# Clearing the second block buffer of a recommendation tower with DMAs from DRAM in place of a ScalarE copy

## The chip, the core and the metric

The kernel runs on one core of a Trainium2 chip. Its engines are TensorE (PE in the profile; PEld is its weight load), VectorE (DVE), ScalarE (ACT), GpSimd (POOL) and SyncE (SP). Each works through its own list of instructions in order, and the lists wait for each other only through semaphores. SP issues the ordinary DMAs, POOL the indirect ones (gathers); both kinds run on the same 16 DMA engines, in queue q1 and queue q0 of the profile. The metric is device time in microseconds of one execution, the median of the runs.

## What is computed

For 512 samples: 50 embedding rows of 16 numbers are looked up, all pairwise inner products of the 50 rows are taken, and these 1225 numbers with 16 dense features go through a three-layer network.

```python
e = jnp.stack([tbl_0[ids[:, 0]], ..., tbl_49[ids[:, 49]]], axis=1)
gram = jnp.einsum('bid,bjd->bij', e, e)
z = gram[:, _I_IDX, _J_IDX]
h = jnp.concatenate([z, dense_ctx], axis=1)
h = jnp.maximum(h @ W_top1 + b_top1, 0.0)
h = jnp.maximum(h @ W_top2 + b_top2, 0.0)
y = h @ W_top3
```

## The kernel before

The samples are worked on in `TILES` = 4 tiles of 128, numbered t = 0 to 3. For each tile:

- **Small tables** (26 of them, and one larger) lie whole in SBUF. ACT makes one-hot rows (`onehots`), PE multiplies them with the tables (`select(t, u)`, `select_big(t)`), and DVE picks the wanted number out of each product (`pick`) and sums it up (`fold`).
- **Large tables** are read with one indirect DMA for each table and tile, issued by POOL: 11 "mid" and 12 "late" gathers for a tile, 92 in all, one after the other and without any wait but that for the ids. They write to `moving`; semaphores `mid_gathered[t]` and `late_gathered[t]` count them. The last six of tile 3 have a semaphore of their own.
- **Turning.** DVE transposes `moving` into `mcols` (`turn_mid(t)`, line 637, after the mid gathers; `turn_late(t)`, line 659, after the late ones) and the small tables' rows into `scols` (`turn_smalls(t)`).
- **Spreading.** The pairwise products of four groups of samples are done in one matmul against a block-diagonal operand, `blocks`, which has room for two tiles: `blocks[:, t % 2]`. Only the four diagonal blocks are ever written after the start (`diagonal`, line 222, called from `spread_mid` and `spread_late`, half by ACT and half by DVE). All the rest of it must be zero, so both halves of `blocks` are cleared once: the one for tiles 0 and 2 by DVE (line 530) and ACT (line 332) at the start, the one for tiles 1 and 3 by ACT alone, in the middle of tile 0's work.
- **Products.** PE multiplies: `product_y(t)` (line 860) after `spread_mid(t)`, `product_x(t)` (line 879) after `spread_late(t)` and ACT's `raise_late(t)` (line 420). ACT and DVE move the results to `z` (`unload_y`, `unload_x`, line 237), and PE runs the network: `first_layer` (line 886) and `second_layer`.

The orders on ACT, DVE and PE are written out by hand; the parts of the four tiles are interleaved. Around the change ACT's list reads

```python
            onehots(1, 1)
            place_lower(0)
            shift(0)
            clear(blocks[:, 1]).then_inc(zeroed[1], 1)
            raise_mid(0)
            spread_mid(0)
            onehots(1, 2)
            spread_late(0, 0, YS)
            raise_late(0, 0, YS)
```

SP's list issues all inputs of the first phase in one run: ids, small tables, the one-hot sources `wide`, `table_big`, 12 pieces of the first weight matrix, and the second layer's weights and biases. Then it waits until ACT is done with `onehots(1, 2)` before it issues the last `wide` load (`load_wide(3)`), for ACT's `onehots(3, 0)` in tile 1's work.

Of the kernel before, what the change touches and what calls it, by code (L numbers as in the profile page):

```python
# [8 lines left out]
P = 128  # L9
# [24 lines left out]
Q = 4  # L34
QP = P // Q
# [11 lines left out]
MS = YS + CH  # L47
# [13 lines left out]
WC = 9  # L61
NWC = -(-NS // WC)
NQ = NS + PARTS
NBC = -(-NQ // BC)
ROUND = 1.5 * 2 ** 23

# [13 lines left out]
def wide_groups(t):  # L80

    return [(NQ * u // NWC, NQ * (u + 1) // NWC) for u in range(NWC)]


def field_groups(size):

    return [(a, min(a + size, NQ)) for a in range(0, NQ, size)]

# [3 lines left out]
    return f if f < NS else W + f - NS  # L92


def build_tower(nc, quotients, ids, ids_t, extra, small, big, w1, w2, b2, w3, consts_in, ident_in, out, *tables):
    f32 = mybir.dt.float32
    bf16 = mybir.dt.bfloat16
    i32 = mybir.dt.int32
# [5 lines left out]
    with ctx:  # L104
        def sb(name, shape, dt=f32):
            return ctx.enter_context(nc.sbuf_tensor(name, shape, dt))
# [4 lines left out]
        def sem(name):  # L111
            return ctx.enter_context(nc.semaphore(name))
# [14 lines left out]
        quot_t = sb("quot_t", [P, B], bf16)  # L127
        wide = sb("wide", [P, 2, NQ * P], bf16)
        quot = sb("quot", [P, TILES, NS])
# [4 lines left out]
        mask_big = sb("mask_big", [P, TILES, BR])  # L134
        onehot = sb("onehot", [P, 2, NQ, P])
        square = sb("square", [P, BC * P])
# [5 lines left out]
        blocks = sb("blocks", [P, 2, QP, MS, Q])  # L142
# [44 lines left out]
        late_cols = sem("late_cols")  # L187
        mid_upper = sem("mid_upper")
        late_upper = sem("late_upper")
        zeroed = [sem(f"zeroed{n}") for n in range(2)]  # L190
        cleaned = sem("cleaned")
        mid_blocks = [sem(f"mid_blocks{n}") for n in range(2)]
        late_blocks = [sem(f"late_blocks{n}") for n in range(2)]
# [26 lines left out]
        def diagonal(copy, t, q, a, b):  # L220

            return copy(blocks[QP * q:QP * (q + 1), t % 2, :, a:b, q], mcols[QP * q:QP * (q + 1), t % 2, :, a:b])  # L222

        def share(t, side):

            n = Q // 2 if t < TILES - 1 else 1
            return range(n) if side == 0 else range(n, Q)
# [23 lines left out]
        @block.sync  # L251
        def _(sp):

            sp.dma_start(ids_sb[:, 0:NL], ids[:, 0:NL]).then_inc(first_loaded, 16)
            sp.dma_start(ids_t_sb[:], ids_t).then_inc(ids_t_loaded, 16)
            sp.dma_start(consts[:], consts_in).then_inc(consts_loaded, 16)
            sp.dma_start(ident[:], ident_in).then_inc(ident_loaded, 16)
            sp.dma_start(ids_sb[:, NL:], ids[:, NL:]).then_inc(ids_loaded, 16)

            def load_table(u):  # L260

                a, b = START[UNITS[u][0]], START[UNITS[u][1]]
                sp.dma_start(table[:, a:b], small[P * a:P * b, :].rearrange("(p c) o -> p (c o)", p=P)
                             ).then_inc(tables_loaded[u], 16)

            def load_wide(t):

                for a, b in wide_groups(t):
                    sp.dma_start(wide[:, t % 2, P * a:P * b], quotients[t:t + 1, P * a:P * b].to_broadcast([P, P * (b - a)])
                                 ).then_inc(wide_loaded[t], 16)  # L270

            for u in range(0, 3):
                load_table(u)
            sp.wait_ge(quot_ready, 1)
            by_field = quotients.rearrange("t (s b) -> s t b", s=NQ)
            sp.dma_start(by_field[0:NS], quot_t[0:NS, :].rearrange("s (t b) -> s t b", t=TILES)).then_inc(quot_stored, 16)
            sp.dma_start(by_field[NS:NQ], quot_t[W:W + PARTS, :].rearrange("s (t b) -> s t b", b=P)
                         ).then_inc(quot_stored, 16)
            for u in range(3, NSC):
                load_table(u)  # L280
            sp.wait_ge(quot_stored, 32)
            load_wide(1)
            for i in range(PARTS):
                sp.dma_start(table_big[:, i], big.rearrange("(i p r) d -> p i (r d)", i=PARTS, r=BR)[:, i]).then_inc(big_loaded, 16)
            load_wide(2)
            for c in range(CH):
                sp.dma_start(w1_sb[:, c], w1.rearrange("(c p) n -> p c n", p=P)[:, c]).then_inc(w1_loaded, 16)
            for side in range(2):
                sp.dma_start(z[SIDE * side + WIDE:SIDE * (side + 1)], extra[side:side + 1, 0:2]).then_inc(extra_loaded[0], 16)
            sp.dma_start(w2_sb[:], w2.rearrange("(k p) n -> p k n", p=P)).then_inc(w2_loaded, 16)  # L290
            sp.dma_start(b2_sb[:], b2.to_broadcast([3 * W, H2])).then_inc(w2_loaded, 16)
            sp.dma_start(w3_sb[:], w3.to_broadcast([P, H2])).then_inc(w2_loaded, 16)
            sp.wait_ge(onehot_ready, NBC + NWC)
            load_wide(3)
            for t in range(2, TILES):
                sp.wait_ge(sums_made, t - 1)
                for side in range(2):
                    sp.dma_start(z[SIDE * side + WIDE:SIDE * (side + 1), t % 2], extra[side:side + 1, t]
                                 ).then_inc(extra_loaded[t - 1], 16)
            sp.wait_ge(y_ready, TILES)  # L300
            sp.dma_start(out.rearrange("(p t) o -> p (t o)", t=TILES), y[:]).then_inc(stored, 16)
            sp.wait_ge(stored, 16)
# [20 lines left out]
        def _(act):  # L323
            def zeros(shape):

                n, m = shape
                return moving[:, 0, 0, 0:D].unsqueeze(1).unsqueeze(1).to_broadcast([P, n, m, D])

            def clear(part):

                to = part.rearrange("p j s q -> p (j s q)").rearrange("p (n m d) -> p n m d", m=2, d=D)
                return nc.scalar.copy(to, zeros((part.shape[1] * MS * Q // (2 * D), 2)))
# [1 line left out]
            act.wait_ge(padded, 1)  # L334
            nc.scalar.copy(fixed[:, :, UPPER:, D:], zeros((2, NS))).then_inc(cleaned, 1)
            nc.scalar.copy(fixed[:, :, 0:UPPER, 0:D], zeros((2, UPPER))).then_inc(cleaned, 1)
            clear(blocks[:, 0, QP // 2:]).then_inc(zeroed[0], 1)
            act.wait_ge(consts_loaded, 16)
            act.wait_ge(ident_loaded, 16)
            nc.scalar.copy(ident_bf[:], ident[:]).then_inc(selector_ready, 1)  # L340
# [44 lines left out]
            def spread_mid(t):  # L385

                act.wait_ge(mid_cols, t + 1)
                if t >= 2:
                    act.wait_ge(y_made, 2 * (t - 1))
                act.wait_ge(zeroed[t % 2], 2 - t % 2)  # L390
                for q in share(t, 0):
                    diagonal(nc.scalar.copy, t, q, YS, MS).then_inc(mid_blocks[0], 1)

# [9 lines left out]
            def spread_late(t, a, b):  # L403

                act.wait_ge(late_cols, t + (2 if a else 1))
                if t >= 2:
                    act.wait_ge(x_made, 2 * (t - 1))
                act.wait_ge(zeroed[t % 2], 2 - t % 2)
                for q in share(t, 0):
                    diagonal(nc.scalar.copy, t, q, a, b).then_inc(late_blocks[0], 1)  # L410

# [50 lines left out]
            onehots(1, 1)  # L462
            place_lower(0)
            shift(0)
            clear(blocks[:, 1]).then_inc(zeroed[1], 1)
            raise_mid(0)
            spread_mid(0)
            onehots(1, 2)
            spread_late(0, 0, YS)
# [46 lines left out]
        def _(dve):  # L516
# [10 lines left out]
            for n in range(3):  # L527
                nc.vector.memset(adder[W * n:W * n + 1], 1.0).then_inc(adder_ready, 1)
            step(nc.vector.memset(quot_t[:], 0.0))
            nc.vector.memset(blocks[:, 0, 0:QP // 2], 0.0).then_inc(zeroed[0], 1)  # L530
            dve.wait_ge(ids_t_loaded, 16)
            dve.wait_ge(consts_loaded, 16)
            step(nc.vector.tensor_scalar(quot_f[:], ids_t_sb[:], iota[0:W + PARTS, 3 + R + BR:4 + R + BR],
# [17 lines left out]
            for left, to, r in ((parts[0][1], masks[0], RS[0]), (parts[1][1], masks[1], RS[1])):  # L551
                n = to.shape[2]
# [86 lines left out]

            def spread_mid(t):  # L640

                dve.wait_ge(zeroed[t % 2], 2 - t % 2)
                dve.wait_ge(mid_cols, t + 1)
                if t >= 2:
                    dve.wait_ge(y_made, 2 * (t - 1))
                for q in share(t, 1):
                    diagonal(nc.vector.tensor_copy, t, q, YS, MS).then_inc(mid_blocks[1], 1)
# [13 lines left out]

            def spread_late(t, a, b):

                dve.wait_ge(zeroed[t % 2], 2 - t % 2)
                dve.wait_ge(late_cols, t + (2 if a else 1))
                if t >= 2:
                    dve.wait_ge(x_made, 2 * (t - 1))  # L667
                for q in share(t, 1):
                    diagonal(nc.vector.tensor_copy, t, q, a, b).then_inc(late_blocks[1], 1)
# [139 lines left out]
        def _(pe):  # L809
# [11 lines left out]
            def select(t, u):  # L821
# [7 lines left out]
                else:  # L829
                    pe.wait_ge(onehot_ready, NBC + NWC * (t - 1) + 1 + sum(end < b for _, end in wide_groups(t)))  # L830
                if t == 0:
# [6 lines left out]
            def select_big(t):  # L838

                m = first_unit(t) + NSC  # L840
                pe.wait_ge(rows_used, m - 1)
                pe.wait_ge(onehot_ready, NBC + NWC * t)
                pe.wait_ge(big_loaded, 16 * PARTS)
# [86 lines left out]
            def second_bias(t):  # L930

                if t == 0:
                    pe.wait_ge(w2_loaded, 48)
                    pe.wait_ge(bcast_used, NBC)
                    pe.wait_ge(bias_parts, 3)
# [172 lines left out]
```

## Time and profile before

| | us |
|---|---|
| median of 3 runs | 134.31 (133.75 to 134.5) |
| the profiled execution, own time | 134.14 |
| its span, first to last instruction | 132.3 |
| busy in the span: PE, PEld | 116.3, 105.6 |
| busy: DVE, POOL, ACT | 90.5, 87.8, 73.1 |

In the page's time line the span is cut into 40 slices of 3.3 us. Each digit is the busy share of a slice in tenths. The DMA row shows that the 16 DMA engines are full in slices 1 to 8 (to about 30 us), half full in slices 9 to 11, and almost empty after. PEclk is the clock that TensorE was granted; it lies lower in slices 8 to 10. A row of a timeline reads: start, duration, engine, line, operation, output<-input, shapes, and in brackets how long the engine had been idle and what released it.

### The profile page before, as it was taken

To read this page: it belongs to the slowest core of one execution; us is meant where nothing else is said; L and a number is where in the kernel's file an instruction comes from. 1 tells how busy PE (TensorE), PEld (TensorE's weight loads), DVE (VectorE), ACT (ScalarE), POOL (GpSimd) and SP (SyncE) were. 2 spreads that over 40 slices of the span, in tenths; PEclk is the share of its full clock that TensorE was granted. 3 is DMA by queue.
4 is the path that set the end of the run, shared out by engine and by line. 5 is a ranking of instruction groups with operands and counts; after the bars stand their busy time and mean duration, and the time that the engine had idled before them with its cause. 6 is when DMAs were issued, how large, how long until landed. Compare 5 with 4: busy or idle time off the path is not lost.

```text
span 132.3 us, 3154 instructions
## 1 busy us (share of the span) xinstructions
PE 116.3 (88%) x1266; PEld 105.6 (80%) x1266; DVE 90.5 (68%) x162; ACT 73.1 (55%) x106; POOL 87.8 (66%) x96
## 2 busy tenths in 40 slices
PE   0199699739999999999989999999989999998990
PEld 0189486529996999999976999997789999898980
DVE  5947857997977789984875599965959635424211
ACT  7765999999699659964521934012930142222210
POOL 2777877877877778777777787787787787750000
PEclk9999999975699999999999999999999999999999
DMA  2999999993530100001011000000010000010000
GB/s 40 260 265 294 380 380 368 373 338 75 185 130 10 10 10 7 5 7 16 5 7 12 5 7 7 10 11 6 9 12 5 7 12 5 7 12 0 5 0 1
DMA packets 9411, 10.92 MB, mean 83 GB/s; under 512 B 2667, under 2 KB 6411, under 8 KB 9395
## 3 DMA queue, kind: packets, MB, share of 16 engines
q1 hardware_dynamic: 6453, 9.96, 22.8%
q0 software_dynamic: 2944, 0.76, 5.7%
q8 instruction: 10, 0.16, 0.5%
q14 instruction: 4, 0.03, 0.1%
HBM read 10.68 MB, written 0.03 MB: 81 GB/s over the span
## 4 chain that ended last, share of the span: by engine, by line
POOL 65%; issue 21%; PE 6%; DMA 3%; DVE 2%; POOLq 1%; DVEq 0%
POOL moving L317 33%; POOL moving L312 32%; DMA moving<-tbl,ids_sb 2%; PE psm L886 2%; PE gram L879 2%; DMA ids_sb<-in_ids 1%; PE pt L949 1%; POOLq L104 1%; DVE blocks L222 1%; PE p L886 1%; PE gram L886 1%; DVE mcols L659 0%; DVE h2w L704 0%; DVEq L667 0%; DVEq L653 0%
## 5 line engine op out<-in xcount | busy, mean ns | idle before, releaser
L317 POOL DMA_INDIRECT moving<-tbl,ids_sb x48 | 45.6, 950 | 14.6 <-issue 14.6
L312 POOL DMA_INDIRECT moving<-tbl,ids_sb x44 | 41.9, 953 | 15.5 <-issue 13.1
L886 PE MATMUL p<-z,w_sb 128*128 128x128 f32 x312 | 38.7, 275 | 0.0
L834 PE MATMUL psm<-table,onehot 128*128 128x160 f32 (+1 forms) x208 | 34.6, 317 | 3.9 <-DVE picked L588 3.3
L886 PEld LDWEIGHTS p<-z,w_sb 128*128 128x128 f32 x312 | 37.0, 192 | 0.8 <-issue 0.4
L834 PEld LDWEIGHTS psm<-table,onehot 128*128 128x128 f32 x208 | 30.6, 208 | 6.2 <-DVE picked L588 4.5
L577 DVE TENSOR_REDUCE fixed<-picked 128x48 f32<-128x480 f32 (+2 forms) x32 | 19.7, 635 | 0.2
L237 DVE COPY z<-gram 63x384 f32<-63x384 f32 (+1 forms) x18 | 9.3, 516 | 10.9 <-PE gram L879 6.8
L588 DVE TENSOR_TENSOR picked<-psm,mask_more 128x480 f32<-128x480 f32 x20 | 13.0, 651 | 5.0 <-PE psm L834 4.8
L222 ACT COPY blocks<-mcols 32x384 f32<-32x384 f32 (+3 forms) x15 | 13.0, 863 | 3.7 <-DVE mcols L659 3.5
L237 ACT COPY z<-gram 63x384 f32<-63x384 f32 (+1 forms) x18 | 7.8, 434 | 12.6 <-PE gram L879 10.0
L626 DVE STREAM_TRANSPOSE scols<-fixed 128x1632 f32<-128x1632 f32 x4 | 12.4, 3089 | 0.0
L363 ACT ACTIVATE onehot<-wide,consts 128x1280 f32<-128x1280 bf16 x9 | 12.2, 1353 | 0.1
L879 PEld LDWEIGHTS gram<-blocks,scols 128*63 128x63 f32 x320 | 9.7, 138 | 2.6 <-issue 2.5
L879 PE MATMUL gram<-blocks,scols 128*63 128x52 f32 (+2 forms) x320 | 10.2, 220 | 1.8 <-DVE blocks L222 1.8
L845 PE MATMUL psm<-table_big,onehot 128*128 128x400 f32 x32 | 11.6, 506 | 0.1
L367 ACT ACTIVATE onehot<-onehot 128x1280 f32<-128x1280 f32 x9 | 11.4, 1271 | 0.3
L222 DVE COPY blocks<-mcols 32x384 f32<-32x384 f32 (+3 forms) x21 | 10.7, 507 | 0.8
L817 PE MATMUL pt<-quot_t,ident_bf 128*128 128x128 bf16 x30 | 3.7, 256 | 7.1 <-ACT ident_bf L340 5.4
L588 DVE TENSOR_TENSOR picked<-psm,mask_less 128x512 f32<-128x512 f32 (+1 forms) x12 | 7.7, 643 | 3.1 <-PE psm L834 2.9
L845 PEld LDWEIGHTS psm<-table_big,onehot 128*128 128x128 f32 x32 | 5.8, 190 | 3.9 <-DVE picked L588 0.3
L860 PE MATMUL gram<-blocks,scols 128*63 128x48 f32 x256 | 8.9, 232 | 0.0
(58 smaller groups left out, 102.7 us busy)
## 6 DMA issues: line engine op xcount, KB each, us to landing
w_sb<-in_w SPq DMA_DIRECT2D x12, 256.0 KB
wide<-quotients SPq DMA_DIRECT2D x9, 320.0 KB, 6.6
moving<-tbl,ids_sb POOLq DMA_INDIRECT x92, 2.4
table<-in_small SPq DMA_DIRECT2D x5, 240.0 KB, 3.6
table_big<-in_big SPq DMA_DIRECT2D x4, 200.0 KB
table<-in_small SPq DMA_DIRECT2D x2, 256.0 KB, 4.9
w_sb<-in_w SPq DMA_DIRECT2D x1, 512.0 KB, 10.0
table<-in_small SPq DMA_DIRECT2D x1, 192.0 KB, 5.1
```

The source lines that it names most:

```text
L222: return copy(blocks[QP * q:QP * (q + 1), t % 2, :, a:b, q], mcols[QP * q:QP * (q + 1), t % 2, :, a:b])
L237: return copy(to.rearrange("p k (n j) -> p k n j", n=2), g[:, 1 + a:1 + b].rearrange("p (k h) n j -> p k h n j", h=2)[:, :, h])
L312: nc.gpsimd.indirect_dma_start(moving[:, t, YS + n, 0:D], None, tables[n - 1], bass.IndirectOffsetOnAxis(ap=large_ids[:, t, n:n + 1], axis=0),
L317: nc.gpsimd.indirect_dma_start(moving[:, t, XS + n, 0:D], None, tables[HALF + n - 1], bass.IndirectOffsetOnAxis(ap=large_ids[:, t, HALF + ...
L363: nc.scalar.activation(onehot[:, t % 2, a:b, :], wide[:, t % 2, P * a:P * b].rearrange("p (f b) -> p f b", b=P), ACT.Square, bias=iota[:, ...
L577: nc.vector.tensor_reduce(fixed[:, t % 2, UPPER + a:UPPER + b, 0:D], picked_small(m, u), AX.X, ALU.add).then_inc(folded, 1)
L588: nc.vector.tensor_tensor(picked_small(m, u), psm[:, m % 2, 0:START[b] - START[a]].rearrange("p (f r d) -> p f d r", f=b - a, d=D), masks[ ...
L626: nc.vector.transpose(scols[:, t % 2, :, 0:MID].rearrange("p j s -> p s j"), fixed[:, t % 2]).then_inc(small_cols, 1)
L834: ins = nc.tensor.matmul(psm[:, m % 2, START[f] - START[a]:START[f + 1] - START[a]], onehot[:, t % 2, f, :], table[:, START[f]:START[f + 1 ...
L845: ins = nc.tensor.matmul(psm[:, m % 2, 0:BR * D], onehot[:, t % 2, NS + i, :], table_big[:, i, :], start=(i == 0), stop=(i == PARTS - 1))
L879: ins = nc.tensor.matmul(gram_out(0, WIDE, g, a, b), scols[:, t % 2, g, XB:], blocks[:, t % 2, g, a:b, :], start=True, stop=True)
L886: return nc.tensor.matmul(hidden_sums(t, k), w1_sb[:, c, P * k:P * (k + 1)], z[:, t % 2, c, :], start=first, stop=last)
```

## The change

ACT no longer clears `blocks[:, 1]`. Eight DMAs on SP's queue copy a row of 400 zeros from DRAM, a new input, to all 128 partitions, each to an eighth of that buffer (400 numbers in a partition, 1600 bytes). They are issued behind the last weights of the second layer and ahead of the wait for `load_wide(3)`. The readers wait for their semaphore `emptied` where they waited for `zeroed[1]`. All other orders stay.

```diff
+CLEARS = 8
@@ build_tower
-        zeroed = [sem(f"zeroed{n}") for n in range(2)]
+        zeroed = sem("zeroed")
+        emptied = sem("emptied")
@@ sync
             sp.dma_start(w3_sb[:], w3.to_broadcast([P, H2])).then_inc(w2_loaded, 16)
+            for n in range(CLEARS):
+                part = blocks[:, 1, QP // CLEARS * n:QP // CLEARS * (n + 1)].rearrange("p j s q -> p (j s q)")
+                sp.dma_start(part, zeros_in.to_broadcast([P, QP // CLEARS * MS * Q])).then_inc(emptied, 16)
             sp.wait_ge(onehot_ready, NBC + NWC)
             load_wide(3)
@@ scalar, spread_mid and spread_late; vector, the same two
-                act.wait_ge(zeroed[t % 2], 2 - t % 2)
+                if t % 2:
+                    act.wait_ge(emptied, 16 * CLEARS)
+                else:
+                    act.wait_ge(zeroed, 2)
@@ scalar, the order
             shift(0)
-            clear(blocks[:, 1]).then_inc(zeroed[1], 1)
             raise_mid(0)
@@ kernel
+        "zeros": np.zeros((1, QP // CLEARS * MS * Q), np.float32),
```

On ACT, between the one-hot rows of tile 1 and the spreading of tile 0, the kernel before has this list (L332 is the clear, L374 to L383 are `place_lower` and `shift`, L400 is `raise_mid(0)`, L222 are the spreads, L363 and L367 are `onehots`):

```order
L374 COPY moving<-fixed 128x12x16
L375 COPY moving<-fixed 128x13x16
L383 COPY fixed<-fixed 128x25x16
L332 COPY blocks<-moving 128x3200
L400 ACTIVATE scols<-mcols,consts 128x32x12
L222 COPY blocks<-mcols 32x32x12 x2
L363 ACTIVATE onehot<-wide,consts 128x1280
L367 ACTIVATE onehot<-onehot 128x1280
L222 COPY blocks<-mcols 32x32x13 x2
L420 ACTIVATE scols<-mcols,consts 128x32x11
```

After the change, at the same place (line numbers have moved):

```order
L380 COPY moving<-fixed 128x12x16
L381 COPY moving<-fixed 128x13x16
L389 COPY fixed<-fixed 128x25x16
L409 ACTIVATE scols<-mcols,consts 128x32x12
L225 COPY blocks<-mcols 32x32x12 x2
L369 ACTIVATE onehot<-wide,consts 128x1280
L373 ACTIVATE onehot<-onehot 128x1280
L225 COPY blocks<-mcols 32x32x13 x2
L432 ACTIVATE scols<-mcols,consts 128x32x11
```

One instruction is gone and nothing else has moved. On SP, from the weights to the end, the kernel before has this list:

```order
L287 DMA w_sb<-in_w 128x512 x12
L289 DMA z<-in_extra 1x3072 x2
L290 DMA w_sb<-in_w 128x4x256
L291 DMA b_sb<-in_b 96x256
L292 DMA w_sb<-in_w 128x256
L269 DMA wide<-quotients 128x1280 x3
L298 DMA z<-in_extra 1x1536 x4
```

And after the change:

```order
L290 DMA w_sb<-in_w 128x512 x12
L292 DMA z<-in_extra 1x3072 x2
L293 DMA w_sb<-in_w 128x4x256
L294 DMA b_sb<-in_b 96x256
L295 DMA w_sb<-in_w 128x256
L298 DMA blocks<-in_zeros 128x400 x8
L272 DMA wide<-quotients 128x1280 x3
L304 DMA z<-in_extra 1x1536 x4
```

The eight new DMAs stand ahead of `load_wide(3)`. The lists of PE, DVE and POOL are the same but for line numbers.

## Rows read from the trace of the kernel before

**Rows 1.** The page: the chain of work that ended last, by engine.

```profile
POOL 65%; issue 21%; PE 6%; DMA 3%; DVE 2%; POOLq 1%; DVEq 0%
```

**Rows 2.** Timeline, POOL: first gather, last late gather of tile 0, last gather.

```profile
2.81 1.08 POOL L312 DMA_INDIRECT moving<-tbl,ids_sb  x1 [2.37 <-DMA ids_sb<-in_ids]
...
30.51 0.94 POOL L317 DMA_INDIRECT moving<-tbl,ids_sb  x1 [0.30 <-issue]
...
117.15 0.94 POOL L317 DMA_INDIRECT moving<-tbl,ids_sb  x1 [0.30 <-issue]
```

**Rows 3.** Timeline of the end, DVE and PE.

```profile
119.49 0.55 DVE L659 STREAM_TRANSPOSE mcols<-moving 128x192 f32<-128x192 f32 x1 [2.15 <-DMA moving<-tbl,ids_sb]
...
120.12 1.06 DVE L222 COPY blocks<-mcols 32x192 f32<-32x192 f32 x3
...
120.91 0.28 PE L938 MATMUL pt<-b_parts,adder 96*128 96x256 bf16 x1
...
121.54 2.02 PE L879 MATMUL gram<-blocks,scols 128*63 128x24 f32 x64 [0.36 <-DVE blocks L222]
```

**Rows 4.** Timeline, ACT, 25 to 37 us.

```profile
25.25 2.85 ACT L332 COPY blocks<-moving 128x3200 f32<-128x3200 f32 x1
...
31.74 1.27 ACT L367 ACTIVATE onehot<-onehot 128x1280 f32<-128x1280 f32 x1
34.31 1.92 ACT L222 COPY blocks<-mcols 32x416 f32<-32x416 f32 x2 [1.30 <-DVE mcols L659]
36.26 0.61 ACT L420 ACTIVATE scols<-mcols,consts 128x352 f32<-128x352 f32 x1
```

**Rows 5.** Timeline, DVE: where it waits for gathers, tiles 0, 1, 3.

```profile
33.30 0.98 DVE L659 STREAM_TRANSPOSE mcols<-moving 128x416 f32<-128x416 f32 x1 [0.95 <-DMA moving<-tbl,ids_sb]
...
46.78 0.91 DVE L637 STREAM_TRANSPOSE mcols<-moving 128x384 f32<-128x384 f32 x1 [1.28 <-DMA moving<-tbl,ids_sb]
...
51.85 1.07 DVE L222 COPY blocks<-mcols 32x384 f32<-32x384 f32 x2
...
63.12 1.00 DVE L659 STREAM_TRANSPOSE mcols<-moving 128x416 f32<-128x416 f32 x1 [0.86 <-DMA moving<-tbl,ids_sb]
...
112.05 0.62 DVE L659 STREAM_TRANSPOSE mcols<-moving 128x224 f32<-128x224 f32 x1 [0.21 <-issue]
```

**Rows 6.** Timeline, PE and weight loads: tile 0, then the later stalls to 107 us.

```profile
26.50 1.08 PE L834 MATMUL psm<-table,onehot 128*128 128x160 f32 x6 [0.94 <-DVE picked L588]
30.00 3.68 PE L834 MATMUL psm<-table,onehot 128*128 128x160 f32 x14 [2.41 <-DVE picked L588]
...
36.31 1.16 PE L834 MATMUL psm<-table,onehot 128*128 128x128 f32 x8
37.40 2.05 PE L879 MATMUL gram<-blocks,scols 128*63 128x52 f32 x64
...
48.23 0.84 PEld L834 LDWEIGHTS psm<-table,onehot 128*128 128x128 f32 x6 [0.33 <-DVE picked L588]
...
66.92 2.05 PE L879 MATMUL gram<-blocks,scols 128*63 128x52 f32 x64 [0.56 <-DVE blocks L222]
...
96.28 2.05 PE L879 MATMUL gram<-blocks,scols 128*63 128x52 f32 x64 [0.52 <-DVE blocks L222]
```

**Rows 7.** Windows: us, PE busy (x), granted clock, DMA share, GB/s.

```profile
28.00:29.00 1.00, 0.00 (x0) 0.69 1.06 331
...
31.00:32.00 1.00, 1.00 (x6) 0.50 0.11 29
...
35.00:36.00 1.00, 1.00 (x38) 0.89 0.88 269
```

**Rows 8.** Gathers, issue to landing: started 8 to 20 us, then 50 to 119.

```profile
DMA to landing us min/median/max: 5.1/5.7/6.4
...
DMA to landing us min/median/max: 2.2/2.3/3.4
```

**Rows 9.** SP's queue: the last issue ahead of the new place.

```profile
22.80 1.08 SPq L292 DMA_DIRECT2D w_sb<-in_w  x1
```

More of the change, by code:

```diff
@@ L92, in quotient_row, with build_tower @@
     return f if f < NS else W + f - NS
-def build_tower(nc, quotients, ids, ids_t, extra, small, big, w1, w2, b2, w3, consts_in, ident_in, out, *tables):
+def build_tower(nc, quotients, ids, ids_t, extra, small, big, w1, w2, b2, w3, consts_in, ident_in, zeros_in, out, *tables):
     f32 = mybir.dt.float32
@@ L336, in _ @@
             nc.scalar.copy(fixed[:, :, 0:UPPER, 0:D], zeros((2, UPPER))).then_inc(cleaned, 1)
-            clear(blocks[:, 0, QP // 2:]).then_inc(zeroed[0], 1)
+            clear(blocks[:, 0, QP // 2:]).then_inc(zeroed, 1)
             act.wait_ge(consts_loaded, 16)
@@ L407, in spread_late @@
                     act.wait_ge(x_made, 2 * (t - 1))
-                act.wait_ge(zeroed[t % 2], 2 - t % 2)
+                if t % 2:
+                    act.wait_ge(emptied, 16 * CLEARS)
+                else:
+                    act.wait_ge(zeroed, 2)
                 for q in share(t, 0):
@@ L529, in _ @@
             step(nc.vector.memset(quot_t[:], 0.0))
-            nc.vector.memset(blocks[:, 0, 0:QP // 2], 0.0).then_inc(zeroed[0], 1)
+            nc.vector.memset(blocks[:, 0, 0:QP // 2], 0.0).then_inc(zeroed, 1)
             dve.wait_ge(ids_t_loaded, 16)
@@ L640, in spread_mid @@
             def spread_mid(t):
-                dve.wait_ge(zeroed[t % 2], 2 - t % 2)
+                if t % 2:
+                    dve.wait_ge(emptied, 16 * CLEARS)
+                else:
+                    dve.wait_ge(zeroed, 2)
                 dve.wait_ge(mid_cols, t + 1)
@@ L662, in spread_late @@
             def spread_late(t, a, b):
-                dve.wait_ge(zeroed[t % 2], 2 - t % 2)
+                if t % 2:
+                    dve.wait_ge(emptied, 16 * CLEARS)
+                else:
+                    dve.wait_ge(zeroed, 2)
                 dve.wait_ge(late_cols, t + (2 if a else 1))
```

## The prediction

> **What bounds the kernel now.** I read the chain of work that ended last first. It is POOL's for 65% of the span, with 21% more of "issue", POOL's gap between two gathers [rows 1]. The timeline shows what that is: 92 gathers, each about 0.94 us and then 0.30 us of gap, from 2.81 us to the last at 117.15 us, with no wait but the first [rows 2]. Only 2.15 us of DMA wait, a transpose, the last spread, the last product and the network's tail come behind [rows 3]. So POOL is a floor: the last gather starts at 117.15 whatever ACT does.
>
> Next I looked for how near PE is to that floor, since PE is busy for 116 of 132 us. At the end PE is free at 121.19 (120.91 + 0.28), and the product starts at 121.54 because it waited 0.36 for DVE's spread, which hangs on the last gather [rows 3]. PE has 0.35 us in hand there. Before that it stood still in only a few places after 37 us, all of them behind DVE and, through DVE, behind gathers: 0.33, 0.56 and 0.52 us [rows 6], and once more in tile 3, where DVE had waited 0.21 us for a gather [rows 5]. So two queues run side by side: whatever makes PE later by more than about 2 us shows in the time, and nothing that makes ACT or PE earlier can show.
>
> **What is removed: 2.85 us of ACT.** The copy at 25.25 [rows 4]. Without it `raise_mid(0)`, `spread_mid(0)` and `onehots(1, 2)` move up, by 2.85 us at most: the one-hot rows of `onehots(1, 2)`, done at 33.01 (31.74 + 1.27) before [rows 4], then come at 30.2 to 33.0. But then ACT stands in front of `spread_late(0)`, which started at 34.31 after 1.30 us of waiting for DVE's transpose [rows 4], and that transpose waited 0.95 us for the gathers of tile 0 [rows 5]. What ACT gains is added to this wait. PE does not use the earlier one-hot rows: it comes to them, in `select(1, 6)`, at 36.31 [rows 6], 3.3 us after they were there. Worth of the removal: 0.
>
> **What is added: eight DMAs.** Each writes 128 x 1600 bytes, together 1.64 MB. SP is free for them from 23.88 (22.80 + 1.08) and then did nothing until ACT released `load_wide(3)` at 33.01 [rows 4, 9], so issuing costs nothing that anybody waits for. The data joins a queue that is already full: before, the DMA engines still carried 331 GB/s at 28 us, with a share above 1, and had fallen to 0.11 at 31 [rows 7]. At 331 GB/s the zeros take 4.9 us, so the engines, which would run dry about 30.3, stay full until about 35. Behind them comes `load_wide(3)`, three times 128 x 2560 bytes, 0.98 MB or another 3.0 us: full until about 38. The zeros are wanted by `spread_mid(1)` on DVE at 51.85 [rows 5]: more than 14 us to spare, so the new wait itself costs 0, and at half that rate, landing about 41, still 0.
>
> **What the added traffic hits.** The gathers. Under full load one took 5.1 to 6.4 us from issue to landing, median 5.7; with empty engines 2.2 to 3.4, median 2.3 [rows 8]. The last late gather of tile 0 starts at 30.51 [rows 2]. In the kernel before that is the moment when the bulk ends, and it was in by 33.30, 2.79 us later, when the transpose started [rows 5]. With the zeros the engines are full for its whole life. The two bounds are 2.8 us (no hindrance) and 6.4; I take the median under load, 5.7, since it stands amid the same kind of traffic. The Trainium skill speaks against the change here: "DMA: Bandwidth & Descriptors", section "Issuing engines are not separate DMA queues", says that DMAs of all issuing engines run on the same 16 engines and interleave. The trace agrees: 5.7 against 2.3 us.
>
> Step by step from there:
> - `turn_late(0)` starts at 30.51 + 5.7 = 36.2, 2.9 later than 33.30.
> - ACT's `spread_late(0)` and `raise_late(0)` follow it without a gap and end at 36.87 + 2.9 = 39.8 [rows 4]. DVE's half is done earlier.
> - PE is done with `product_y(0)` at 36.3 as before, waits about 1.2 us until DVE has picked (behind the transpose, about 1.3 us after its start), does `select(1, 6)` in 1.16 us [rows 6], and waits again, about 1.4 us. Stalled products started 0.35 us after the copy they waited for (121.19 to 121.54) [rows 3], so `product_x(0)` starts at 40.1, 2.7 later than 37.40 [rows 6].
> - Then the stalls give time back. 0.33 us at 48.23 [rows 6]: DVE was 1.28 us early there for a gather [rows 5]. 0.56 at 66.92 [rows 6]: DVE had 0.86 in hand at 63.12 [rows 5]. 0.52 at 96.28 [rows 6]. 0.21 at 112.05 [rows 5], where DVE's own reserve ends first. 0.35 at 121.19 [rows 3]. Together 1.97.
> - Left: 2.7 - 1.97 = about 0.7 us at the end.
>
> Made against the profiled execution's own time this is 134.14 + 0.7 = 134.9; the median of the runs shown is 0.17 above that execution, so 134.31 + 0.7 = **135.0 us**. By the two ends of the landing under load: 5.1 us gives 0.1, 134.4; 6.4 gives 1.4, 135.7. A difference of 0.5%, 0.67 us, is about what a measurement of this kernel can tell from no change, and my sum lies on that line.
>
> **The rivals.**
> 1. *The gathers are hardly hindered, or it is all absorbed; no change, 134.3.* For it: the delay must reach 2.2 us before anything shows, and reserves that the rows don't show can only add to 1.97. It would do if the engines let the small packets of the gathers by. Against it: 5.1 us is the least that was seen once the engines were full. A rule of the Trainium skill would put the time here: "DMA: Bandwidth & Descriptors", section "Queues, rings and completion order", has each DMA engine take turns between queues, a packet at a time, so that a gather should wait for a packet or two of the bulk and not for its whole backlog; no run here shows the turns themselves. As a mechanism of this kernel: a gather lands below 5 us under load, DVE is less than 2.2 us late, the end stays at 134.3.
> 2. *TensorE's clock falls a second time; slower.* PE stood still for 0.94 us up to 26.50, worked for 1.08, and stood still again for 2.41 us [rows 6]; in the first half of that second gap the granted clock fell from full to 0.50, where it was until 35 [rows 7]: 1.2 in place of 2.4 GHz. My forecast has PE stand still for 1.2 and 1.4 us between 36.3 and 40.1, which is not so different. At half clock some 7 us of PE work is done at half speed, 3.4 us lost, all beyond the reserves: 134.3 + 0.7 + 3.4 = 138.4. Against it: neither gap is as long as the 2.41 us of then, and the work between and after is dense.
> 3. *Faster: the freed 2.85 us reach the end.* This would need ACT and not the gathers to set `spread_late(0)`, and PE's later stalls not to hang on gathers: then up to 2 us, 132.3. It decides at the transpose at 33.30: had it not waited for a DMA, ACT's earlier hand would count. It did wait, and the last gather at 117.15 stays. A gain over 0.5% is then left only to a shorter tail or a lucky median.
> 4. *The zeros land late.* If they came in only after 51.85, `spread_mid(1)` would wait; with `load_wide(3)` behind them. Every us beyond counts for both engines. It needs a rate below 77 GB/s (1.64 MB from 30.5 to 51.85) against the 331 seen. At 60 GB/s they come at 57.8, 6 us late; the stalls from 66.92 on give 1.64 back, and the time is 138.6.
>
> **How the numbers follow.** Forecast as worked out, delay with most of it absorbed: 0.50, of it 0.20 below the line of 0.67 us and 0.30 above. Rival 1: 0.27, of it 0.01 on each side by the spread of medians. Rival 2: 0.13. Rival 3: 0.07. Rival 4: 0.03. Slower by over 0.5%: 0.30 + 0.13 + 0.03 + 0.01 = 0.47. Within 0.5%: 0.20 + 0.25 = 0.45. Faster: 0.08. The range takes in rival 1 with a little below it for the spread of medians, 134.0, and the upper end of the forecast with some room for gathers slower than any seen, 136.2; the clock rival and most of the faster one are left out.
>
> **What would show it.** In the profile of the changed kernel: the DMA share near 1 until 35 us or more. `turn_late(0)` starting near 36.2 with a longer wait for a DMA; if it stands at 33.5, rival 1 holds and the time must be 134.3. `product_x(0)` near 40, two PE stalls of 1.2 to 1.4 us ahead of it. The stalls at 48, 67 and 96 us gone, and the last product 0.7 us late and released by PE's own queue. The granted clock between 36 and 45: 1.00, or rival 2. POOL's pace of 1.25 us unchanged; if the added traffic slowed its issue, each 0.01 us on the 70 gathers behind would add 0.7 us, and the prediction would be wrong for a reason of its own. It would be wrong as well if `onehots(1, 2)` ending earlier let PE skip ahead somewhere that I took as DVE's.

## The result and the profile after

The changed kernel takes 141.67 us (141.26 to 142.17), the kernel before 134.07 in the same measurement: ratio 1.057, 95% interval 1.054 to 1.060. It is 7.6 us slower, far above the 135.0 that was forecast and the 136.2 of the range. Most runs of the experiments below fell in measurements where every kernel, the one before included, took 239 to 248 us, with ACT, DVE and PE standing still for up to 37 us at a time until POOL's last gather near 117 us: of those only the rates and landings of DMAs are read, and only g1 and m1 compare in time with the 134 us.

The page of the changed kernel: span, the two rows of the time line that changed, and the chain that ended last.

```profile
span 140.2 us, 3161 instructions
...
PEclk9999999975865589999999999999999999999999
DMA  2999999984446700100010100001000000000000
...
PE 66%; POOL 15%; DMA 10%; issue 6%; DVE 1%; DVEq 0%
```

The chain was POOL's [rows 1]; now it is PE's, and DMA's 10% is nearly all one wait. The DMA row shows the first surprise: after slice 8 (slices are counted from 0) the engines are not full, as forecast, but at 0.4 for three slices and at 0.6 and 0.7 for two. Windows of it, columns as in [rows 7]:

```profile
33.00:34.00 1.00, 1.00 (x6) 0.50 0.40 127
38.00:39.00 1.00, 0.00 (x0) 1.00 0.46 118
40.00:41.00 1.00, 0.00 (x0) 0.50 0.46 138
48.00:49.00 1.00, 1.00 (x24) 0.50 0.63 214
50.00:51.00 1.00, 1.00 (x22) 1.00 0.08 8
```

Timeline of the changed kernel: SP's issues of the zeros and of `wide`, DVE's transpose of tile 0's late gathers, and PE behind it.

```profile
23.40 8.75 SPq L298 DMA_DIRECT2D blocks<-in_zeros  x8
32.19 4.88 SPq L272 DMA_DIRECT2D wide<-quotients  x3
...
43.63 0.95 DVE L673 STREAM_TRANSPOSE mcols<-moving 128x416 f32<-128x416 f32 x1 [10.92 <-DMA moving<-tbl,ids_sb]
...
45.12 2.08 PE L851 MATMUL psm<-table,onehot 128*128 128x128 f32 x8 [7.97 <-DVE picked L599]
47.20 3.31 PE L896 MATMUL gram<-blocks,scols 128*63 128x52 f32 x64
50.44 0.94 PE L851 MATMUL psm<-table,onehot 128*128 128x128 f32 x6
```

`turn_late(0)` starts at 43.63 in place of 33.30 [rows 5], after 10.92 us of waiting for gathers. PE stands still for 7.97 us and `product_x(0)` starts at 47.20 in place of 37.40 [rows 6]. How long transfers took from issue to landing, for the issues between 30 and 33 us, and the one DMA wait of the chain:

```profile
wide<-quotients SPq DMA_DIRECT2D x1, 320.0 KB, 14.8
blocks<-in_zeros SPq DMA_DIRECT2D x1, 200.0 KB, 17.5
moving<-tbl,ids_sb POOLq DMA_INDIRECT x3, 12.5
...
30.89 12.64 DMA moving<-tbl,ids_sb
```

The columns are engine, operation and count, KB, and the median landing; the last row has start and duration. The last late gather of tile 0 started at 30.89, 0.38 later than before [rows 2], and landed after 12.64 us. With the rows the 7.9 us of span add up: `product_x(0)` 9.80 late; it ran at half clock, 3.31 us in place of 2.05 [rows 6], so what follows it is 9.80 + 1.26 = 11.06 late; 2.39 is given back on the way to the last product, which starts at 130.21 against 121.54 and is 8.67 late (the 2.39 is the remainder of these two; PE has no stall left behind 50 us); and the store of `y` landed 0.8 us sooner (below). 9.80 + 1.26 - 2.39 - 0.8 = 7.87.

### The profile page after: what moved, and what is told of

Read it like the earlier page. It is cut to its first block, busy times and chain, and to the rows that moved or that the text cites. A ratio compares the mean times of both kernels' runs of the same rounds, so it can differ in the third digit from the quotient of the medians.

```text
span 140.2 us, 3161 instructions
## 1 busy us (share of the span) xinstructions
PE 118.9 (85%) x1266; PEld 108.4 (77%) x1266; DVE 90.1 (64%) x162; ACT 70.4 (50%) x105; POOL 87.9 (63%) x96
## 4 chain that ended last, share of the span: by engine, by line
PE 66%; POOL 15%; DMA 10%; issue 6%; DVE 1%; DVEq 0%
PE p L903 25%; PE psm L851 12%; DMA moving<-tbl,ids_sb 9%; PE gram L896 8%; POOL moving L318 8%; POOL moving L323 7%; PE psm L862 6%; PE pt L966 5%; PE gram L877 4%; PE psm L903 4%; PE gram L903 2%; DMA ids_sb<-in_ids 1%; PE pt L955 0%; DVE picked L599 0%; DVE h2w L721 0%
## 5 line engine op out<-in xcount | busy, mean ns | idle before, releaser
L851 PE MATMUL psm<-table,onehot 128*128 128x160 f32 (+1 forms) x208 | 35.8, 326 | 11.7 <-DVE picked L599 11.3
L851 PEld LDWEIGHTS psm<-table,onehot 128*128 128x128 f32 x208 | 31.9, 217 | 13.9 <-DVE picked L599 12.2
L896 PEld LDWEIGHTS gram<-blocks,scols 128*63 128x63 f32 x320 | 10.9, 152 | 0.9 <-ACT scols L432 0.3
L896 PE MATMUL gram<-blocks,scols 128*63 128x52 f32 (+2 forms) x320 | 11.5, 235 | 0.0
L673 DVE STREAM_TRANSPOSE mcols<-moving 128x416 f32<-128x416 f32 (+2 forms) x5 | 4.1, 818 | 11.0 <-DMA moving<-tbl,ids_sb 10.9
```

What stands on the lines that cost most here:

```text
L851: ins = nc.tensor.matmul(psm[:, m % 2, START[f] - START[a]:START[f + 1] - START[a]], onehot[:, t % 2, f, :], table[:, START[f]:START[f + 1 ...
L896: ins = nc.tensor.matmul(gram_out(0, WIDE, g, a, b), scols[:, t % 2, g, XB:], blocks[:, t % 2, g, a:b, :], start=True, stop=True)
```

## The experiments

Each time stands beside that of the kernel before in the same measurement. GB/s are of all DMA traffic in a window, the gathers' few included.

**Each partition its own row (e1, again as f1 and g1).** The place, the count and the bytes of the DMAs stay; the source is 128 different rows.

```diff
-                sp.dma_start(part, zeros_in.to_broadcast([P, QP // CLEARS * MS * Q])).then_inc(emptied, 16)
+                sp.dma_start(part, zeros_in).then_inc(emptied, 16)
-        "zeros": np.zeros((1, QP // CLEARS * MS * Q), np.float32),
+        "zeros": np.zeros((P, QP // CLEARS * MS * Q), np.float32),
```

> The zeros come from an array of 128 rows in DRAM, a row of its own for each partition, in place of one row read 128 times; the eight DMAs still share that array. Place and size are the same. Theory A (the one row of 1600 bytes is what makes the transfer slow: all DMA engines read the same few addresses, 107 to 125 GB/s): the zeros run at 330 GB/s or more, the DMA share is near 1 until about 35 us, the last late gather of tile 0 lands about 5.7 us after its start, turn_late(0) starts near 36.2, the time is 134.5 to 136. Theory B (slow because DMAs into blocks, or issued at this place, are slow, wherever they read from): the DMA share stays near 0.4, turn_late(0) near 43, time 141 to 142.

> The kernel with 128 rows of zeros, one for each partition, again, on a chip where the kernel before takes 134 us. Theory A (the single row is slow to read): DMA share near 1 until about 35 us, turn_late(0) starts near 36.2, 134.5 to 136 us; by the steps of the prediction 135.0. Theory B (the place or the target is slow): turn_late(0) near 43, 141 to 142 us.

> The kernel with 128 rows of zeros, one for each partition. In the two sets before this one every kernel, the one before the change too, took 240 to 247 us, so they do not compare with the 134 us that the change was measured against. If the kernel before takes 134 us here: theory A (the single row is slow to read) has turn_late(0) near 36.2 and 134.5 to 136 us, by the steps of the prediction 135.0; theory B (the place or the target is slow) has turn_late(0) near 43 and 141 to 142 us.

e1 and f1 gave 246.4 and 246.0 us beside 247.0 and 246.5, with 292 to 353 GB/s from 30 to 34 us; behind that e1 had 160 to 170 from 34 to 38 us, so the full rate did not hold to the end there. g1 gave 133.12 us beside 134.07: ratio 0.993, interval 0.990 to 0.995. Timeline of g1, DVE and PE, then two of its windows:

```profile
35.88 0.98 DVE L673 STREAM_TRANSPOSE mcols<-moving 128x416 f32<-128x416 f32 x1 [2.98 <-DMA moving<-tbl,ids_sb]
...
39.48 2.05 PE L896 MATMUL gram<-blocks,scols 128*63 128x52 f32 x64 [0.91 <-ACT scols L432]
...
121.33 2.03 PE L896 MATMUL gram<-blocks,scols 128*63 128x24 f32 x64
...
35.00:36.00 1.00, 1.00 (x24) 0.50 1.07 392
37.00:38.00 1.00, 0.86 (x15) 1.00 0.72 253
```

From 32 to 37 us the traffic is 370 to 392 GB/s and the engines are full. Up to tile 0's product this is the chain that the prediction described: transpose at 35.88 (forecast 36.2), `product_x(0)` at 39.48 (40.1), behind one stall of 0.91 us in place of the two of 1.2 and 1.4, and the clock at 1.00 from 37 us on. The end is not: the last product starts at 121.33, 0.2 before the 121.54 of the kernel before, where the forecast had it 0.7 late, and the time lies 1.4 us below theory A's 134.5. Theory A holds in its mechanism and missed in its time; B falls. The bytes, the place, the target and the wait for `emptied` are as in the change, so none of these made the 7.6 us: the single row did.

**A row for each of the eight DMAs (e2, again as f2 and h1).**

```diff
-                sp.dma_start(part, zeros_in.to_broadcast([P, QP // CLEARS * MS * Q])).then_inc(emptied, 16)
+                sp.dma_start(part, zeros_in[n:n + 1].to_broadcast([P, QP // CLEARS * MS * Q])).then_inc(emptied, 16)
-        "zeros": np.zeros((1, QP // CLEARS * MS * Q), np.float32),
+        "zeros": np.zeros((CLEARS, QP // CLEARS * MS * Q), np.float32),
```

> Eight rows of zeros in DRAM, each DMA reads one of its own for all 128 partitions. Theory A1 (any single row read by 128 partitions is slow): as the changed kernel, turn_late(0) near 43, 141 to 142 us. Theory A2 (slow only because all eight DMAs, so all packets in flight, hit one row): faster by several us, near the kernel with 128 rows, 135 to 137. Theory B (the place or the target): 141 to 142.

> Eight rows, one for each DMA, read by 128 partitions, again. Theory A1 (any row read by 128 partitions at a time is slow): as the changed kernel, 141 to 142. Theory A2 (slow only when all packets in flight read one row): the earlier look had 283 and 262 GB/s while the zeros ran, so near the kernel with own rows, 134.5 to 136, turn_late(0) at 35.5 to 37.5.

> Eight rows of zeros in DRAM, each of the eight DMAs reads one of its own for all 128 partitions. The kernel with 128 rows took 133.1 us beside 134.1, the changed kernel with one row 141.7. Theory A1 (any single row read by 128 partitions is slow): about 141.7, turn_late(0) near 43. Theory A2 (slow only when all packets in flight read one row): 133 to 134.5, turn_late(0) at 35.5 to 37.5, DMA share near 1 until about 36 us.

245.0, 244.8 and 246.4 us beside 247.0, 246.5 and 246.5. Between the two theories: 210 to 274 GB/s at 32 to 36 us in e2 and f2, 255 falling to 138 in h1, above one row, and below the own rows of g1. Windows of h1 (us, granted clock, DMA share, GB/s):

```profile
32.00:34.00 2.00, 0.50 0.81 255
36.00:38.00 2.00, 0.50 0.67 149
38.00:40.00 2.00, 0.50 0.73 138
```

Eight rows help, and in h1 less at the end; that fewer DMAs are in flight there would explain it, but was not shown. What this is worth in time stays open.

**One row of 2560 bytes, five DMAs (e3, again as f3).** A DMA writes 640 numbers to each partition.

```diff
-CLEARS = 8
+CLEARS = 5
-                part = blocks[:, 1, QP // CLEARS * n:QP // CLEARS * (n + 1)].rearrange("p j s q -> p (j s q)")
-                sp.dma_start(part, zeros_in.to_broadcast([P, QP // CLEARS * MS * Q])).then_inc(emptied, 16)
+                part = blocks[:, 1].rearrange("p j s q -> p (j s q)")[:, 640 * n:640 * (n + 1)]
+                sp.dma_start(part, zeros_in.to_broadcast([P, 640])).then_inc(emptied, 16)
-        "zeros": np.zeros((1, QP // CLEARS * MS * Q), np.float32),
+        "zeros": np.zeros((1, 640), np.float32),
```

> One row of 640 zeros (2560 bytes, the size of a row of wide), five DMAs in place of eight; the bytes are the same. Theory A (the same addresses for everybody): still slow, somewhat less since a packet is longer: rate 110 to 190 GB/s, turn_late(0) 39 to 43, 138 to 142 us. Theory C (it is the size or alignment of the 1600 byte packets, since the broadcasts of wide with 2560 bytes ran at 390 GB/s in the kernel before): 330 GB/s, 134.5 to 136 us.

> One row of 2560 bytes, five DMAs, again. Theory A2: all packets in flight read one row, so still slow, 160 to 170 GB/s by the earlier look; 1.64 MB take about 10 us, turn_late(0) 38 to 42, 137 to 141 us. Theory C (the 1600 byte packets): 134.5 to 136.

246.5 and 244.8 us beside 247.0 and 246.5. Windows of e3, same columns:

```profile
32.00:34.00 2.00, 0.50 1.06 170
34.00:36.00 2.00, 0.50 0.86 170
36.00:38.00 2.00, 0.50 0.94 169
```

170 GB/s is 66 readings of the row in a us. The row of 1600 bytes is read at 103 to 123 GB/s (the changed kernel in windows of 2 us, 32 to 38 us), 64 to 77 readings. `wide` has packets of the same 2560 bytes and ran at 390 GB/s in the kernel before (36 to 37 us). So the length of the packets is not the cause (theory C falls), and the rate grows with it.

**Behind `load_wide(3)` (e4, again as f4).** The loop of eight DMAs moves, one row as in the change.

```diff
+            sp.wait_ge(onehot_ready, NBC + NWC)
+            load_wide(3)
             for n in range(CLEARS):
                 part = blocks[:, 1, QP // CLEARS * n:QP // CLEARS * (n + 1)].rearrange("p j s q -> p (j s q)")
                 sp.dma_start(part, zeros_in.to_broadcast([P, QP // CLEARS * MS * Q])).then_inc(emptied, 16)
-            sp.wait_ge(onehot_ready, NBC + NWC)
-            load_wide(3)
```

> The eight DMAs of the one row stand behind load_wide(3), so they start after 31 us, when the gathers of tile 0 are nearly all issued. Theory G (the loss is the late landing of tile 0's gathers): turn_late(0) starts between 33.5 and 38 in place of 43.6; what then limits is the slow transfer beside the gathers of tile 1, wanted at 46.8, and the zeros themselves, wanted at 51.9 and landing about 52 to 56; 135 to 140 us, below the changed kernel. Rival theory W (the wait for the zeros, emptied, costs the time): as slow as the changed kernel or slower, 141.5 or more, since the zeros come later.

> The one row of 1600 bytes, behind load_wide(3), again. Theory G (late gathers of tile 0 are the loss): turn_late(0) starts between 33.5 and 38 in place of 43.6; then the gathers of tile 1, wanted at 46.8, or the zeros, wanted at 51.9, limit; 135 to 140 us. Theory W (waiting for the zeros costs the time): 141.5 or more.

242.1 and 247.0 us beside 247.0 and 246.5, so neither G nor W is decided in time. But here the zeros ran when no gather did, right behind a broadcast of `wide`. Windows of e4, same columns:

```profile
145.00:146.00 1.00, 0.50 1.00 366
146.00:147.00 1.00, 0.90 1.02 395
...
148.00:149.00 1.00, 1.00 1.11 83
149.00:150.00 1.00, 1.00 0.94 118
```

The three DMAs of `wide`, each reading a row of 2560 bytes of its own, run at 366 to 395 GB/s; then the one row of zeros at 83 to 118, at first with a DMA share as high as before, and at 117 GB/s with a share of 0.30 from 153 to 155 us. So the share does not tell whether the engines are held up. A broadcast in itself is not slow, and by g1 neither is `blocks` as a target: what is left is that all engines read one place in DRAM. f4 has 123 GB/s at 156 us.

**One row of 12800 bytes, one DMA (i1, again as j1, k1 and m1).** The same two lines of the program then make one DMA.

```diff
-CLEARS = 8
+CLEARS = 1
```

> One row of 3200 zeros (12800 bytes) and one DMA in place of eight; the bytes stay. In the traces so far one row of 1600 bytes was read at 107 to 123 GB/s, 67 to 77 readings in a us, and one of 2560 bytes at 170, 66 readings. Theory R (a place in DRAM is handed out about 70 times in a us, whatever the length): 128 readings take 1.9 us, so this no longer limits, and the zeros run at 300 GB/s or more; turn_late(0) 35.5 to 37, 133 to 135 us where the kernel before takes 134. Theory S (all engines on one small area of DRAM is what is slow, by bytes): 110 to 180 GB/s, turn_late(0) 39 to 44, 138 to 142.

> One row of 3200 zeros and one DMA, again, for its time on a chip where the kernel before takes 134 us. The look before had the zeros at 383 GB/s, as theory R (a place in DRAM is handed out about 70 times in a us) would have it. Theory R then: turn_late(0) at 35.5 to 37, 133 to 135 us. If the loss has another cause than the rate of the zeros, 138 us or more in spite of that rate.

> One row of 3200 zeros and one DMA, once more for its time, if the kernel before takes 134 us here. Theory R (a place in DRAM is handed out about 70 times in a us): turn_late(0) at 35.5 to 37, no second fall of the clock, the last product within 0.5 us of the 121.54 of before, 133.5 to 134.5 us. If the loss has another cause than the rate of the zeros, 138 or more.

> One row of 3200 zeros and one DMA, for its time where the kernel before takes 134 us. Theory R: turn_late(0) at 35.5 to 37, 133.5 to 134.5 us. Another cause than the rate of the zeros: 138 or more.

i1, j1 and k1: 244.4, 242.9 and 245.9 us beside 246.7, 245.7 and 245.2, with 286 to 394 GB/s from 30 to 34 us. m1: 137.36 us beside 134.08, ratio 1.026, interval 1.021 to 1.031. Theory R (a place in DRAM is handed out about 70 times in a us, whatever the length) was right on the rate and wrong on the time, and the other cause, which had 138 or more, is not met either. Timeline of m1, DVE and PE, then its windows:

```profile
38.13 0.95 DVE L673 STREAM_TRANSPOSE mcols<-moving 128x416 f32<-128x416 f32 x1 [5.94 <-DMA moving<-tbl,ids_sb]
...
26.47 1.08 PE L851 MATMUL psm<-table,onehot 128*128 128x160 f32 x6 [0.91 <-DVE picked L599]
29.91 2.28 PE L851 MATMUL psm<-table,onehot 128*128 128x160 f32 x14 [2.36 <-DVE picked L599]
...
41.71 3.66 PE L896 MATMUL gram<-blocks,scols 128*63 128x52 f32 x64
45.30 0.97 PE L851 MATMUL psm<-table,onehot 128*128 128x128 f32 x6
...
125.13 2.02 PE L896 MATMUL gram<-blocks,scols 128*63 128x24 f32 x64
...
28.00:29.00 1.00, 0.00 (x0) 1.00 1.11 349
35.00:36.00 1.00, 0.00 (x0) 1.00 1.00 385
39.00:40.00 1.00, 0.37 (x1) 0.50 0.21 41
```

The zeros are as fast as in g1, and yet the transpose starts at 38.13, 2.3 us later than there: the gathers issued between 29.5 and 31 us landed after 7.2 us (median) here and 5.6 in g1. The rows copied, which the profile counts as packets, are 12800 bytes in place of 1600. `product_x(0)` starts at 41.71, 4.3 late, and it runs at half clock: 3.66 us in place of 2.05. So PE is 4.31 + 1.61 = 5.92 us late behind it; the last product is 3.59 late (125.13 against 121.54 [rows 3]), 2.33 given back, and the span is 3.3 longer. Without the half clock it would be some 1.7 longer by this sum (an estimate). I hold the packets' length for the reason of the later landing; it was not varied by itself. In m1 SP had also issued all zeros by 23.82, where the eight DMAs of g1 left it between 23.64 and 30.71, so more of them could stand ahead of the last gathers; no run separates the two.

**The row of zeros as an input that nothing reads, ACT clears as before (i2, again as j2, k2 and n1).** The diff is against the kernel before.

```diff
-def build_tower(nc, quotients, ids, ids_t, extra, small, big, w1, w2, b2, w3, consts_in, ident_in, out, *tables):
+def build_tower(nc, quotients, ids, ids_t, extra, small, big, w1, w2, b2, w3, consts_in, ident_in, zeros_in, out, *tables):
+        "zeros": np.zeros((1, 400), np.float32),
```

> The kernel before with the row of zeros as an input that nothing reads: ACT still clears. In every profile with that input the last DMA, the store of y, landed 1.4 us after its issue, and in the one of the kernel before 2.2. Theory P (the new input moves the output to another place in DRAM, and the store lands sooner there): 1.4 us for the store, 133.3 us beside 134.1. Theory Q (the store's landing has to do with the DMAs of zeros or varies by itself): 2.2 us and 134.1, or no pattern.

> The kernel before with an input of zeros that nothing reads, again. Its store landed 1.4 us after its issue on the chip of the look before, as in every profile with this input and no other. Theory P (placement of the output): 0.8 us less than the kernel before, 133.3 beside 134.1. Theory Q: 134.1.

> The kernel before with the unused input, once more. Theory P (placement of the output): the store lands after 1.4 us, 133.3 beside 134.1. Theory Q: 2.2 us, 134.1.

> The kernel before with an input of zeros that nothing reads, beside the kernel before at 134.1. In the three looks so far its store landed 1.4 us after its issue; in the kernel before it was 2.2. Theory P (the new input moves the output to another place in DRAM): 133.3 us, a ratio near 0.994. Theory Q (the 0.9 us by which own rows beat the kernel before come from the earlier ACT): 134.1, ratio 1.000.

246.0, 244.7, 244.0 and 245.2 us beside 246.7, 245.7, 245.2 and 247.0: no time to compare with 134. The store of `y`, issue to landing, in the kernel before, then in n1, g1 and m1:

```profile
y_out<-y SPq DMA_DIRECT2D x1, 2.0 KB, 2.2
```

```profile
y_out<-y SPq DMA_DIRECT2D x1, 2.0 KB, 1.4
```

```profile
y_out<-y SPq DMA_DIRECT2D x1, 2.0 KB, 1.4
```

```profile
y_out<-y SPq DMA_DIRECT2D x1, 2.0 KB, 2.0
```

It was 1.4 us in all fifteen profiles with an input whose rows are 400 or 640 zeros, whether DMAs read it or not and whatever the rest did, 1.8 to 2.0 in the four with a row of 3200, 2.2 in the one without. So theory P holds in that the landing goes with the input and not with the DMAs that read it; that the output's place in DRAM is the reason was not shown, and the 2.2 rests on one profile. g1's span is 1.0 us shorter than that of before, and 0.8 of it is this.

## Why the prediction was wrong

- **What bounds the kernel: right.** Taking 2.85 us from ACT was worth nothing: ACT waited 13.09 us for the transpose in place of 1.30. In g1, where all else was undisturbed, the last product moved by 0.2 us. POOL's pace stayed at 1.25 us, and its last gather started at 117.26, where it was 117.15.
- **The new wait: right.** The zeros landed 10.0 to 17.5 us after their issue, the last at about 47.5, and were wanted at 62.7 in the changed kernel.
- **The step that failed: "At 331 GB/s the zeros take 4.9 us".** They ran at about 120 GB/s and took some 16 us, from 31 to 47.5, the last of them beside `wide`. I had set the rate from the mixed traffic before, without asking where it is read from. Even the broadcasts of `wide` read three places in DRAM; the eight DMAs of the change read one. My slow case, half that rate, was still too fast, and I used it only for the wait for the zeros and not for the gathers.
- **So the landing of a gather was mis-sized: 5.7 us, at most 6.4, against 12.64.** These figures were measured beside traffic of 217 to 393 GB/s (8 to 20 us of the kernel before). Bytes moved from a gather's start to its landing, an estimate from the windows' rates: about 1.5 MB for the last late gather of tile 0 in the changed kernel (12.64 us), 1.9 in g1 (5.41 us), 2.6 in m1 (7.68 us). The rate differs by a factor of three and the bytes by less than two, so I read the landing as a wait for bytes already queued, which grows as their rate falls. This is argued; no run varied the queue alone. I had taken the time as given.
- **A reading that was wrong: "5.1 us is the least that was seen once the engines were full".** It holds from 8 to 20 us only. In the kernel before, the gathers at 4.20 and 5.45 landed after 3.8 and 3.9 us with the DMA share at 0.90 to 1.06 from 4 to 9 us. SP had been issuing for only 4 to 5 us then, so a full share alone does not make a gather late.
- **The chain behind it: right, and its size nearly.** 2.9 us late at the transpose, 2.7 at the product, 1.97 given back was the forecast; g1 had 2.6 and 2.1 and lost nothing at the end. What was given back came to 2.29 in g1, 2.33 in m1 and 2.39 in the changed kernel, so the 1.97 was some 0.4 too small. By the prediction's own sum a landing of 12.64 has the transpose at 30.51 + 12.64 = 43.15, 9.85 late, the product 9.65 late, and 9.65 - 1.97 = 7.7 at the end: 142.0. That this is so near 141.67 is partly luck, since it leaves out the half clock (1.26 more), the store (0.8 less) and the 0.4.
- **Rival 2, the clock: happened, and cost less than priced.** The granted clock fell to 0.50 between 39 and 40 us, while PE stood still (from 37.2 to 45.1), and came back at 50. I had priced 3.4 us; it was 1.26, since PE stood still through most of the stretch, and only `select(1, 6)`, hidden under ACT's copies, and `product_x(0)` (3.31 in place of 2.05 us) ran in it.
- **Rival 1 by the page's rule: fell here.** It had a gather land in less than 5 us under load, and the last late gather of tile 0 took 12.64, and 5.41 beside own rows. Landings below 5 us beside nearly full engines do occur: 3.8 us near 4 us in the kernel before, 4.92 in m1 for the gather at 32.86. The rule in the Trainium skill's "DMA: Bandwidth & Descriptors", section "Queues, rings and completion order", is that an engine changes queues only between packets; its packet is a group of descriptors, which need not be what the profile counts as one. No run here shows these turns. The later gathers of m1 are in line with longer packets, and a wait of a packet or two, if a packet is one row, does not fit the 12.64 us.
- **Rivals 3 and 4: did not happen.** g1 is 0.7% faster, and of its 1.0 us of span 0.8 is the store. The zeros' 120 GB/s stayed above the 77 below which `spread_mid(1)` would have waited.

## What to carry to other kernels

A transfer that nobody waits for can still cost: ask which small transfers share its engines and who waits for those. A broadcast of one short row from DRAM ran here at some 70 readings of the row in a us, whether it had 1600 or 2560 bytes. Beside gathers that somebody waits for, the fill was best from rows of its own for each partition (133.12 us; one long row 137.36; one short row 141.67; ScalarE's own copy 134.07), so such a fill gains next to nothing over an engine that has idle time. When a landing time is taken from a trace, take with it the rate of the traffic it was measured beside.

## What was not expected of the hardware

- One row in DRAM read by 128 partitions at a time: 1600 bytes mostly at 99 to 127 GB/s, with single microseconds at 47 to 85; 2560 at 170; three rows together 366 to 395; 12800 bytes 336 to 390 (m1, 31 to 36 us).
- The DMA share was 0.4 beside 120 GB/s in the changed kernel and near 1 at the same rate in e4, so it did not tell how much was waiting.
- The landing of a 2 KB store was 1.4 us in place of 2.2 with an input that nothing reads.
- The clock did not follow the length of PE's stalls alone. In m1 it stayed at 1.00 through the stalls of 0.91 and 2.36 us near 27 and 29 us, where in the kernel before [rows 6, 7] and in g1 (0.82 from 29 to 30 us, 0.50 behind) it fell within the second of two such stalls.
